# The product with the values, moved from behind the odd step's scores to behind the even step's unit

## What is computed

```python
x = x + attn_a(layernorm(x));  x = x + ffn(layernorm(x))
x = x + attn_b(layernorm(x));  x = x + ffn(layernorm(x))

def attn_a(x):                       # B, S, D = 4, 512, 256; 16 heads of 16
    Q, K, V = (x @ W.T + b).reshape(B, S, 16, 16).transpose(0, 2, 1, 3)   # each with its own W, b
    scores = einsum('bhqd,bhkd->bhqk', Q, K) / sqrt(16)
    out = einsum('bhqk,bhkd->bhqd', softmax(scores), V)
    return out.transpose(0, 2, 1, 3).reshape(B, S, D) @ Wo.T + bo
```

## Time and profile before

| | us |
|---|---|
| three runs | 585.0, 585.2, 585.33 |
| median | 585.2 |
| the profiled execution | 586.36 |
| its span, first to last instruction | 584.6 |
| the loop of 128 steps, first scores to the last product with the values | 45.95 to 253.4 |

### The profile page before, as it was taken

The page is one execution under the profiler, slowest core; times in us unless marked ns, Lnnn a source line. Parts: engine busy times, 40 slices in busy tenths (PEclk is TensorE's granted clock), DMA queues, the critical chain, the costliest instruction groups (busy, mean ns, idle before and its releaser), DMA issues.

```text
span 584.6 us, 8872 instructions
## 1 busy us (share of the span) xinstructions
PE 566.8 (97%) x3288; PEld 390.0 (67%) x3288; DVE 378.0 (65%) x720; ACT 298.3 (51%) x546; POOL 176.7 (30%) x193
## 2 busy tenths in 40 slices
PE   9899999999999998999999999999999999999997
PEld 5534334344434432468988888898777888888887
DVE  5398898888888799735453544558887436344333
ACT  3238778876887687752334232244445233424221
POOL 3955436354545342730101010014333010101000
PEclk9899999999999999999999999999999999999999
DMA  7754741240033030010000000000000010010101
GB/s 232 148 90 155 200 122 35 67 130 26 2 110 109 2 147 3 3 72 2 1 0 1 1 0 1 2 2 0 1 0 2 1 36 1 1 36 2 38 0 37
DMA packets 17924, 26.54 MB, mean 45 GB/s; under 512 B 2585, under 2 KB 10777, under 8 KB 17497
## 3 DMA queue, kind: packets, MB, share of 16 engines
q1 hardware_dynamic: 16024, 24.13, 13.7%
q10 hardware_dynamic: 1856, 1.84, 1.6%
HBM read 10.88 MB, written 5.24 MB: 28 GB/s over the span
## 4 chain that ended last, share of the span: by engine, by line
PE 86%; DVE 5%; ACT 4%; issue 2%; DMA 1%; POOL 1%; SPq 1%; DVEq 0%; ACTq 0%
PE PS L282 83%; PE PS L293 2%; DVE mxr L876 2%; DMA ring<-ql 1%; ACT PR L750 1%; DVE PR L1041 1%; ACT xf L659 1%; ACT qf L673 1%; DVE XNs L857 1%; ACT PR L803 1%; POOL xTl L1072 1%; ACT xTh L659 1%; PE PS L473 1%; DVE AOl L868 1%; SPq L214 1%
## 5 line engine op out<-in xcount | busy, mean ns | idle before, releaser
L282 PE MATMUL PS<-xTh,ring 128*128 128x512 f32 x608 | 188.8, 393 | 0.0
L876 DVE TENSOR_REDUCE mxr<-PS 128x1 f32<-128x512 f32 x256 | 162.9, 681 | 31.1 <-PE PS L282 30.9
L750 ACT ACTIVATE PR<-PS 128x512 f32<-128x512 f32 x256 | 137.9, 605 | 39.9 <-PE PS L282 39.9
L282 PEld LDWEIGHTS PS<-xTh,ring 128*128 128x128 f32 x608 | 113.2, 188 | 23.6 <-issue 1.7
L282 PE MATMUL PS<-xTl,ring 128*128 128x512 f32 x304 | 110.3, 391 | 0.4 <-POOL xTl L1072 0.4
L282 PE MATMUL PS<-ring 48*128 48x512 f32 (+1 forms) x512 | 98.4, 451 | 5.4 <-DVE mxr L876 4.9
L990 DVE TENSOR_TENSOR PR<-PR,PS 128x512 f32<-128x512 f32 x64 | 43.7, 683 | 90.9 <-PE PS L282 73.0
L282 PEld LDWEIGHTS PS<-ring 50*128 50x128 f32 (+1 forms) x512 | 41.3, 185 | 84.9 <-ACT PR L750 57.6
L659 ACT ACTIVATE AOh<-PR 128x512 fp32r<-128x512 f32 x72 | 45.5, 632 | 101.9 <-DVE PR L990 89.9
L1072 POOL TENSOR_TENSOR xTl<-xf,xTh 128x512 fp32r<-128x512 f32 x30 | 43.2, 1457 | 140.0 <-ACT xTh L659 140.0
L868 DVE TENSOR_TENSOR AOl<-PR,AOh 128x512 fp32r<-128x512 f32 x72 | 51.0, 709 | 50.3 <-ACT AOh L659 50.3
(11 more groups left out here) (99 smaller groups left out, 623.6 us busy)
## 6 DMA issues: line engine op xcount, KB each, us to landing
ring<-qh SPq DMA_DIRECT2D x52, 128.0 KB, 3.1
ring<-ql SPq DMA_DIRECT2D x26, 128.0 KB, 3.1
ring<-weight_scratch SPq DMA_DIRECT2D x3, 1024.0 KB, 4.8
weight_scratch<-in_w SPq DMA_DIRECT2D x2, 1024.0 KB, 6.7
X<-in_x SPq DMA_DIRECT2D x3, 512.0 KB, 5.4
out<-X SPq DMA_DIRECT2D x6, 256.0 KB, 2.2
PR<-in_w SPq DMA_DIRECT2D x1, 1024.0 KB, 8.0
ring<-AOh SPq DMA_DIRECT2D x8, 128.0 KB, 4.5
```

The source lines that it names most:

```text
L282: return nc.tensor.matmul(dst, lhsT, rhs, start=start, stop=stop, skip_group_check=True)
L750: nc.scalar.activation(PR[:, j % 8, :], PS[:, kq_bank(j), :], ACT.Exp, scale=HD ** -0.5)\
L876: nc.vector.tensor_reduce(mxr[:, S % 2, blk, TT * p + t:TT * p + t + 1], PS[:, QK0 + i % 3, :], AX.X, ALU.max, negate=True).then_inc(max_d ...
```

## The change

```diff
                 shared_bank(K, b, s)
-                if K % 2 and K >= 3:
-                    weigh_values((K - 3) // 2)
+                if K % 2 == 0 and K:
+                    weigh_values(K // 2 - 1)
```

## The result

| | before | changed |
|---|---|---|
| median of four runs, us | 585.1 (584.91 to 585.33) | 612.84 (610.86 to 613.4) |
| profiled execution, us | 586.36 | 613.17 |
| its span, us | 584.6 | 611.3 |

The changed kernel is slower by 4.7%: ratio 1.0468, 95% interval 1.0443 to 1.0492, or +27.7 us. The forecast was 609.1, in a range of 600 to 617.

The account below looks back on a forecast made before the run. PE was taken to set the pace, with little slack on DVE and ACT. Terms 23.0 - 4.1 - 0.6 + 2.0 + 0.7 + 2.9 gave +23.9 us on the median 585.2, thus 609.1 us, range 600 to 617.

Parts of the forecast that it names:

- (a): Merged score blocks, where a unit stood between an even and an odd step: +0.51 us at 45 places, +23.0 us.
- (b): The product with the values behind a unit: no extra cost and no wait for exponentials.
- (c): Small transposes at s = 5, 13, 21, 29 now stand inside a merged block's wait: -4.1 us.
- (d): Score blocks in two batches that waited for DVE (0.99, not 0.67): DVE has caught up, -0.6 us.
- (e): Product opening a group waits for DVE's read-out in three places without a unit, +2.0 us; behind a unit hidden.
- (f): Maxima's way into `ring` by DMA: hidden in batches with units; two last-batch places without a unit wait, +0.7 us.
- sign against (f): Waits for the maxima's DMA in batches with units, adding up to 0.5 in each of 13 places.
- (g): Loop's end: products wait for exponentials of the step just before, and ACT gets gaps: +2.9 us, from 0 to 4.
- Rival D: Waits of 0.4 throughout the loop drop the clock to 1.2 GHz for a tenth: +20 more, 630 us; chance 0.05.
- A: Merging pays: two steps' scores in a row cost 1.11, not 1.34, giving 571 us; chance 0.04.
- B: No change: the wait lies where PE waited in any case, 585 us; chance 0.03.
- C: DVE and ACT begin blocks rested, first maximum 0.25 sooner, so (a) is half: 598 us; chance 0.10.

Follow-up runs that it names:

- half-tile pair: Kernel of before and changed kernel, each with maxima and exponentials on 256 of 512 columns: 579.61 and 589.75 us.
- one batch alone: Changed order in the second batch only, order of before elsewhere: 591.19 us against 585.11, ratio 1.0104.
- the end alone: Order of before up to step 113, changed order from step 114 on: 590.26 us, ratio 1.0080.
- the end given back: Changed order up to step 114, order of before from step 117 on: 606.19 us, ratio 1.0357.

## Why the prediction was right, point by point

- **(a)** Right in mechanism and size. The row of the last batch that showed a merged pair was the price nearly everywhere: 1.84 and 3.73 for the forecast 1.85 and 3.74, and 1.91 in four pairs of the second and third batch. The half-tile pair shows why, one batch alone shows that it adds up.
- **(b)** The product behind a unit costs 1.00 (52.50 to 53.50). Right.
- **(c), (d)** The transposes vanished inside the block (53.50 to 55.34 is 1.84). They had cost more than (c) took off. It counted 0.21 for each and the six waits of 0.20 that the trace names; but the scores ahead of each of the twelve took 0.94 or 0.85 and not 0.67. By the blocks the gain is 5.2 us, not 4.1. The late blocks of (d), 0.99 in the kernel before (143.88 and 198.41), are gone: -0.6, as forecast.
- **(e)** Forecast: the product at +2.67 in three places. Measured: +2.63 in the first batch (75.84 to 78.47) and twice in the last. Its label in the trace is ACT, and the run with the earlier read-out shows that it is DVE. Behind a unit it was to be hidden by 0.1. At step 26 of the second and third batch it is not: at step 25 DVE also adds a residual (line 936) between the two maxima, and the product waits for the read-out. The unit takes 1.31 to that product (152.54 to 153.85) and not 0.91; twice 0.4 is +0.8 that the sum did not have.
- **(f)** Forecast: 2.20 from scores to product in two places. Measured 2.11 (235.99 to 238.10) and 2.24. A third was overlooked, step 24 of the first batch, which has no unit at step 22 either: 86.75 to 89.05, 2.30, +0.45. The label says ACT; by the times it is the DMA, issued at 85.70 and, with the 2.58 of the earlier trace rows, landed at 88.28, just ahead of the scores at 88.39. Together +1.1, not +0.7. Such waits came at the start of each batch too (0.35 at 102.04), which the forecast had named as a sign against (f); they are hidden in the pair, 1.85 (100.95 to 102.80).
- **(g)** Forecast +2.9, from 0 to 4. Measured 3.2 by the blocks at full clock, and 3.7 by the one execution of the end alone whose clock stayed up.
- **Rival D** came true in part, and that is where the 3.8 us between forecast and result lie. The step that failed is in its weighing: it asked whether the waits of 0.4 in the merged blocks lower the clock, found from the earlier trace rows that they don't, which held, and never asked it of the longer waits that (g) itself had put at the end (0.94 us as measured). The order is such that PE idles nearly half of 4 us there, and the low clock behind it cost 4.06 us by the blocks. Without them the stretches of the table sum to 27.9 - 4.1 = 23.8, against the forecast's 23.9.
- **How much of that is luck.** The main term is not: the changed order without the end costs 606.19 - 585.11 = 21.1 us, and the sum without (g) is 21.0. That it fits to 0.1 is: 1.1 us too little was taken off in (c), and 0.8, 0.4 and 0.3 too little was put on in (e), (f) and (g). And the range does not follow from its parts, which would give 602 to 619 added up straight; the result lies inside either.
- **Rivals A, B, C** did not come: the rows that read x8 take 1.84 like the others, and no last half came at +1.2.

## What to carry to other kernels

Two blocks that need the same few banks are cheapest when other work of PE stands between them: price the merged pair from a place of the trace where it occurs already, start to start, and count the places. Where a consumer's order leaves only one block ahead of the engine that feeds it, look for the latency of that engine in every round, and ask for each new idle stretch of PE what the granted clock will do there, not only for the commonest one. Filler that shortens nothing can pay when it covers such a stretch (3.2 us here); the order of before at the same place was worth 6.6.

## What the runs showed of the hardware that was not expected

- The clock fell to the 1.2 GHz level for about 10 us behind a stretch of 4 us with PE busy for 2.12, and did not fall in 61 us with PE busy for 56. With PE busy for 4.28 of 5 us it held (the end given back). Whether it falls differs between executions of one kernel: 588.85 us at a mean clock of 1.000 and 591.98 at 0.991. Ahead of the loop it fell in the profiled execution of the kernel before, behind one wait of 2.02 us (0.66 over 25 to 30 us), and not in that of the changed kernel, whose wait at the same place was 1.34.
- Halving the columns of a maximum moves the next product in its bank by 0.27 us only (+1.41 to +1.14): 0.72 us of a bank's round trip are the product, its signal, the start of the maximum and the signal back, with full tiles and with half.
- A small transpose, a product of 128 columns, takes 0.20 us to the next block (161.05 to 161.25), and nothing where PE is about to wait for a bank (the scores of two steps take 1.84 us with it, 53.50 to 55.34, and without it, 49.77 to 51.61).
